# Turning tokens and attention by transfers inside SBUF and 32x32 transposes on VectorE, in the first phase of a decoder layer

## The reference

```python
q = elu(x @ Wq.T) + 1; k = elu(x @ Wk.T) + 1; v = x @ Wv.T        # 16 heads of 32
kv_state = einsum('bhnd,bhne->bhde', k, v)
attn_out = einsum('bhnd,bhde->bhne', q, kv_state) / max(q . k.sum(2), 1e-06)
local = xp[:, :-2] * conv_w[:, 0] + xp[:, 1:-1] * conv_w[:, 1] + xp[:, 2:] * conv_w[:, 2] + conv_b
out = (attn_out + local) @ Wp.T + bp
```

## Time and profile before

| | us |
|---|---|
| median of 3 runs (3150.09 to 3150.97) | 3150.3 |
| span of the profiled execution | 3149.0 |
| TensorE busy in it | 3109.7 |
| VectorE, ScalarE, GpSimd busy | 1781.6, 1298.2, 838.2 |
| one step of the first phase | 54.5 |

### The profile page before, as it was taken

The page is one execution under the profiler, slowest core; times in us unless marked ns, Lnnn a source line. Parts: engine busy times, 40 slices in busy tenths (PEclk is TensorE's granted clock), DMA queues, the critical chain, the costliest instruction groups (busy, mean ns, idle before and its releaser), DMA issues.

```text
span 3149.0 us, 41123 instructions
## 1 busy us (share of the span) xinstructions
PE 3109.7 (99%) x15828; PEld 2625.5 (83%) x15828; DVE 1781.6 (57%) x3901; ACT 1298.2 (41%) x2475; POOL 838.2 (27%) x699
## 2 busy tenths in 40 slices
PE   8999999999989999999999989999999999999999
PEld 7888888888878888888888878888888888888887
DVE  6666665766587877877787766232232232221355
ACT  4333333333456666766666653222222222221243
POOL 0101010110146666666666650000000000000144
PEclk9999999999999999999999999999999999999999
DMA  3121121212232112221221232000011000010386
GB/s 111 41 70 51 46 75 41 81 41 94 69 102 82 62 62 82 69 69 56 95 69 55 81 108 81 27 27 27 27 36 45 27 27 28 27 54 17 123 291 227
DMA packets 118802, 220.76 MB, mean 70 GB/s; under 512 B 7504, under 2 KB 13648, under 8 KB 118608
## 3 DMA queue, kind: packets, MB, share of 16 engines
q1 hardware_dynamic: 118608, 218.14, 20.4%
HBM read 152.06 MB, written 66.06 MB: 69 GB/s over the span
## 4 chain that ended last, share of the span: by engine, by line
PE 96%; DVE 2%; issue 1%; ACT 1%; DMA 0%; POOL 0%; SPq 0%; DVEq 0%; ACTq 0%
PE c_p L130 11%; PE c_p L132 11%; PE c_p L131 11%; PE a_p L130 6%; PE a_p L132 6%; PE a_p L131 5%; PE b_n L132 5%; PE b_n L130 5%; PE b_n L131 4%; PE b_t L1597 3%; PE d_p L132 2%; PE d_p L131 2%; PE d_p L130 2%; PE a_r L130 2%; PE a_r L132 2%; PE a_p L902 2%
## 5 line engine op out<-in xcount | busy, mean ns | idle before, releaser
L1217 POOL TENSOR_SCALAR b_soft<-b_soft,b_one_in_sum 128x512 f32<-128x512 f32 x256 | 401.4, 1569 | 299.6 <-DVE b_one_in_sum L1400 299.6
L1817 ACT ACTIVATE c_gate<-c_p,c_bias 128x512 f32<-128x512 f32 x180 | 124.2, 690 | 718.3 <-PE c_p L132 718.3
L1851 DVE TENSOR_TENSOR c_gate<-c_gate,c_gate 128x512 f32<-128x512 f32 x64 | 44.3, 692 | 524.0 <-ACT c_gate L1817 524.0
L1419 DVE TENSOR_TENSOR b_p_lo<-b_t,b_p_hi 128x512 fp32r<-128x512 f32 x256 | 175.2, 684 | 158.9 <-ACT b_p_hi L1274 156.3
L1265 ACT ACTIVATE b_soft<-b_soft,b_minus_top 128x512 f32<-128x512 f32 x256 | 185.2, 724 | 180.9 <-DVE b_minus_top L1411 176.3
L344 POOL TENSOR_TENSOR kept_scale<-c_ln_ve,minus_half 128x4 f32<-128x4 f32 x16 | 16.1, 1009 | 896.5 <-DVE c_ln_ve L336 896.5
L551 ACT ACTIVATE a_elu<-a_p 128x512 f32<-128x512 f32 x128 | 76.6, 599 | 353.1 <-PE a_p L132 353.1
L344 POOL TENSOR_TENSOR a_ln_sc<-a_ln_ve,minus_half 128x4 f32<-128x4 f32 x16 | 16.3, 1017 | 695.3 <-DVE a_ln_ve L336 695.3
L1274 ACT ACTIVATE b_p_hi<-b_t 128x512 fp32r<-128x512 f32 x256 | 151.9, 593 | 107.4 <-PE b_t L1597 107.4
L1411 DVE CUSTOM_DVE_ANT_0 b_soft<-b_l,b_mask_row 128x512 f32<-128x512 f32 x256 | 175.3, 685 | 0.0
L1597 PE MATMUL b_t<-ident,b_soft 128*128 128x128 f32 x1024 | 154.4, 273 | 12.4 <-DVE b_p_lo L1419 11.3
(11 more groups left out here) (286 smaller groups left out, 9622.8 us busy)
## 6 DMA issues: line engine op xcount, KB each, us to landing
a_res<-in_x SPq DMA_DIRECT2D x16, 1024.0 KB, 6.3
x<-a_res SPq DMA_DIRECT2D x16, 1024.0 KB, 5.3
b_mem<-in_ctx SPq DMA_DIRECT2D x16, 1024.0 KB, 5.4
b_x<-x SPq DMA_DIRECT2D x16, 1024.0 KB, 5.6
b_res<-x SPq DMA_DIRECT2D x16, 1024.0 KB, 5.6
x<-b_res SPq DMA_DIRECT2D x16, 1024.0 KB, 4.5
c_x<-x SPq DMA_DIRECT2D x16, 1024.0 KB, 5.9
d_x<-x SPq DMA_DIRECT2D x16, 1024.0 KB, 5.6
```

The costliest lines, as they stand in the source:

```text
L1217: pool.tensor_scalar(soft[:, at, :], soft[:, at, :], one_in_sum[:, at:at + 1], None, ALU.mult).then_inc(p_norm.sem, p_norm.unit)
L1419: dve.tensor_tensor(part.low, pT_bank[:, :].rearrange("p (i s) -> p i s", i=T), part.high_f32(), ALU.subtract).then_inc(p_lo.sem, p_lo.unit)
L1817: act.activation(gate[j % 2][i][:, :], gating.banks[(3 * j + i) % 6][:, :], ACT.Tanh if g == "c" else ACT.Sigmoid, bias=added[:, i, j:j + ...
```

## The change

Transposes on TensorE stay for the weights and the first item. The tokens of the later items and the attention of every item are turned in two moves. First sixteen transfers inside SBUF (`shuffle`), issued by SP, each of 32 partitions by 4 by 128 elements, exchange the 32-row blocks between the partition groups: the block of rows r and columns q goes to rows q. Then VectorE transposes squares of 32x32 inside each partition group (`turn_squares`), 128x512 in one instruction, four for an item. It reads every fourth element of a row, so the channels of a chunk are no longer neighbours: the channel of partition p and chunk c is 4p + c. So that weights and convolution parameters fit, TensorE reads the raw weights and the first item with the same stride (`interleaved`, `spread`). Transposed tokens lie in SBUF (`turned_f`) instead of in PSUM, from where ScalarE and VectorE read them. The transposed attention is written to `z_sum` and the local part added there in place. Both rotas lose the transposes' four places, and SP's stream gets the batches; in step 15 the loads of the second phase stand behind the attention's batch.

```diff
+def interleaved(row, c, chunks):
+
+    return row.rearrange("p (m c) -> p c m", c=chunks)[:, c]
+
...
         for o in range(self.C):
-            mm = pe.transpose(bank[:, o * P:(o + 1) * P], self.stages[i % len(self.stages)][:, o, c * P:(c + 1) * P], self.ident[:, :])
+            raw = self.stages[i % len(self.stages)]
+            part = interleaved(raw[:, o, :], c, self.C) if i in self.spread else raw[:, o, c * P:(c + 1) * P]
+            mm = pe.transpose(bank[:, o * P:(o + 1) * P], part, self.ident[:, :])
...
+    def shuffle(self, sp, to, src, event):
+
+        for q in range(4):
+            for r in range(4):
+                sp.dma_start(to[32 * q:32 * (q + 1), :, r * P:(r + 1) * P],
+                             src[32 * r:32 * (r + 1), :, q * P:(q + 1) * P]).then_inc(event.sem, event.unit)
+
+    def turn_squares(self, dve, to, src, c):
+
+        blocks = src[:, :, :].rearrange("p t (n c) -> p c (t n)", c=self.C)[:, c]
+        return dve.transpose(to[:, c, :], blocks)
...
-            att = sb("att", [P, BLOCKS, P])
+            att = sb("att", [P, T, D])
...
+            def shuffle(sp, b):
+                sp.wait_ge(N.normed.sem, N.normed.upto(b))
+                if b >= 2:
+                    sp.wait_ge(squared.sem, squared.upto(b - 2))
+                self.shuffle(sp, x_shuffled, x, shuffled)
...
-                         + [(kv_sb, g, 0) for g in range(2)] + [(tap2, c, -1) for c in range(C)], B)
+                         + [(kv_sb, g, 0) for g in range(2)], B)
...
-                          [(att_sb, g, 1) for g in range(GROUPS)] + [(z_f, c, 1) for c in range(C)] + [(x1_sb, t, 1) for t in range(T)], B)
+                          [(att_sb, g, 1) for g in range(GROUPS)] + [(x1_sb, t, 1) for t in range(T)], B)
...
-                    if new and new.b == B - 2:
+                    if old:
+                        sp.wait_ge(att_sb.sem, att_sb.upto(old.b))
+                        if old.b >= 1:
+                            sp.wait_ge(attT.sem, attT.upto(old.b - 1))
+                        self.shuffle(sp, att_shuffled, att, att_moved)
+                    if following(new, B):
+                        shuffle(sp, new.b + 1)
+                    if new and new.b == B - 1:
+                        sp.wait_ge(shuffled.sem, shuffled.upto(B - 2))
+                        self.b_load_mem(sp, 0)
+                        sp.wait_ge(tap2.sem, tap2.upto(B - 1))
+                        self.b_load_scale(sp)
+                        sp.wait_ge(squared.sem, squared.upto(B - 2))
                         self.b_load_output_weight(sp)
-                    if new and new.b == B - 1:
-                        sp.wait_ge(xT_ps.sem, xT_ps.upto(B - 1))
-                        self.b_load_mem(sp, 0)
-                        self.b_load_scale(sp)
...
                 def tokens_high(b, c):
-                    act.wait_ge(xT_ps.sem, xT_ps.upto(b, c))
+                    if b == 0:
+                        act.wait_ge(xT_ps.sem, xT_ps.upto(0, c))
+                    else:
+                        act.wait_ge(squared.sem, squared.upto(b - 1, c))
...
-                    act.activation(xT.high[:, c, :], first.bank(b - 1, TURN + c)[:, :], ACT.Copy).then_inc(xT_hi.sem, xT_hi.unit)
+                    act.activation(xT.high[:, c, :], turned(b, c), ACT.Copy).then_inc(xT_hi.sem, xT_hi.unit)
...
+                        dve.wait_ge(att_moved.sem, att_moved.upto(old.b))
                         for c in range(C):
-                            dve.wait_ge(attT_ps.sem, attT_ps.upto(old.b, c))
-                            dve.wait_ge(tap2.sem, tap2.upto(old.b, c))
                             if c >= 2 or old.b >= 1:
                                 dve.wait_ge(z_lo.sem, z_lo.upto(*divmod(old.b * C + c - 2, C)))
-                            dve.tensor_tensor(z_sum[c % 2][:, :], second.bank(s, TURNED + c)[:, :], local[old.par][:, c, :], ALU.add).then_inc(z_f.sem, z_f.unit)
+                            squares = att_shuffled[:, :, :].rearrange("p t (n c) -> p c (t n)", c=C)[:, c]
+                            dve.transpose(z_sum[c % 2][:, :], squares).then_inc(attT.sem, attT.unit)
+                            dve.wait_ge(attT.sem, attT.upto(old.b, c))
+                            dve.wait_ge(tap2.sem, tap2.upto(old.b, c))
+                            dve.tensor_tensor(z_sum[c % 2][:, :], z_sum[c % 2][:, :], local[old.par][:, c, :], ALU.add).then_inc(z_f.sem, z_f.unit)
                             if c >= 1:
                                 z_low(c - 1)
                         z_low(C - 1)
+                    if after:
+                        dve.wait_ge(shuffled.sem, shuffled.upto(after - 1))
+                        for c in range(C):
+                            self.turn_squares(dve, turned_f, x_shuffled, c).then_inc(squared.sem, squared.unit)
...
-                        if old:
-                            turn_att(c)
...
-                    if following(new, B):
-                        for c in range(C - 1 if old else C):
-                            turn_x(new.b + 1, c)
                     if new and old:
                         for t in range(T):
                             output(pe, old.b, t)
-                            if following(new, B) and t == 0:
-                                turn_x(new.b + 1, C - 1)
```

More of the change, by code:

```diff
@@ L357, in turn, with turn_interleaved @@
         return mm
+    def turn_interleaved(self, pe, bank, src, c):
+        for t in range(self.T):
+            mm = pe.transpose(bank[:, t * P:(t + 1) * P], interleaved(src[:, t, :], c, self.C), self.ident[:, :])
+        return mm
+    def shuffle(self, sp, to, src, event):
[6 more added lines that the diff above has]
+        return dve.transpose(to[:, c, :], blocks)
     def token_rows(self, dram, b):
@@ L410, in phase_a @@
             k = sb("k", [P, T, D])
+            self.place = Place(nc, self.base + 1024 * 166)
             kv_mask = sb("kv_mask", [P, 2, KVW])
@@ L959, in phase_b @@
             k_f = sb("k_f", [P, T, HD])
-            mask_u8 = [sb(f"mask_u8{i}", [P, S], U8) for i in range(2)]
+            mask_place = Place(nc, self.base + 1024 * 196)
+            mask_u8 = [mask_place.tile(f"b_mask_u8{i}", [P, S], U8) for i in range(2)]
             mask_row = [sb(f"mask_row{i}", [P, S]) for i in range(2)]
```

78 lines of the change are left out of this document (41 added, 37 removed).

## The result

The changed kernel took 3187.5 us (median of four runs, 3187.2 to 3189.7), the kernel before 3150.6 beside it. The ratio is 1.0117, with a 95% interval of 1.0103 to 1.0131: slower by 37 us, where I had forecast 46 us faster, 3105 us, and a range that ended at 3161. The profiled execution spans 3187.9 us, 38.9 more than before. Lines have moved: an attend is L896 now, a KV product L957, the second half of an elu L724, the z addition L794, its low part L785, the GpSimd additions L578, an issue of a 64 KB transfer L376.

A forecast was written before the change was run, and what follows sets the result against it. TensorE's instruction stream was taken to bound the steady steps. Terms: -53.6 us of transposes, +7.0 at the end, +1.0 at the start, so 3150.3 - 45.6 = 3104.7, rounded 3105 us; own range 3096 to 3113, 8-in-10 range 3096 to 3161.

The forecast's parts named there:

- What TensorE saves: Transposes leaving TensorE's stream save 3.58 us in each of steps 1 to 14, 53.6 us in all before the drain.
- The price of an issue: SP issues each 64 KB transfer in 0.47 us, so sixteen take 7.5 us and a batch 9.5 us with landing.
- The upper bound of 0.69: Slowest issue of a 64 KB transfer, if a 512-byte packet costs 87 ns: 3.8 us wait per step, 3161 us.
- The far case of 0.95: Transfers hardly overlap: 12.1 us wait per step, 3282 us; all of slower together has a chance of 0.22.
- The price of a transpose: A 32x32 transpose over 512 columns on VectorE takes 0.61 us, eight of them 4.9 us per step.
- the bound of 1.45: Upper bound in us for a VectorE transpose, what a normalisation takes while GpSimd runs.
- So I cost steps 1 to 15 at no new wait: The elu of Q ends at 36.1 us of the step, 2.0 us before the second KV group needs it.
- Rivals 1 and 2: First: steps wait for slow transfers, 3161 to 3282 us, chance 0.22. Second: slow transposes lose part of the gain, 3128, 0.16.
- The end: In the drain the attention batch and z chain have no products to hide under: costs 7.0 us.
- The start and step 15: Step 0 saves 1.64 us and strided reads cost 1 (0 to 5); step 15 saves 1.88 at no cost.
- the cover that I had taken as enough: Step 15: memory item lands near 27.5 us, ScalarE lets V copies through before Q units 2 and 3 need banks.
- At 0.67 the whole gain is gone: With 0.67 us per issue, the wait per step and the longer end use up the whole gain.

The follow-up runs named there:

- e12: e9 with one edit: GpSimd does its four residual additions behind the z chain instead of right behind its DMA issues; 3099.4 us, 0.9834.
- e3: The changed kernel with half the rows per transfer, 32 KB in 64 runs instead of 64 KB in 128; 3180.1 us, 1.0089.
- e10: The changed kernel with each 64 KB transfer over all 128 partitions, one run of 512 bytes on each; 3185.2 us, 1.0112.
- e4: The changed kernel with VectorE's transposes reading 512 neighbouring elements instead of every fourth of 2048; 3147.8 us, 0.9992.
- e2: The changed kernel with 24 identity transposes on TensorE behind the first KV group, to fill the wait; 3172.8 us, 1.0071.
- e11: The kernel before with only a stall added: VectorE does three idle transposes ahead of the elu steps of Q in steps 1 to 14; 3212.1 us, 1.0199.
- e8: The changed kernel with the elu steps of Q ahead of VectorE's token transposes and the last item's attention turned by TensorE; 3119.5 us, 0.9900.
- e5: The changed kernel with GpSimd issuing the last eight transfers of every batch, ahead of its norm power; 3163.7 us, 1.0038.
- e9: e8 with half of each batch issued by GpSimd, behind its norm power; 3143.9 us, 0.9979.

## Why the prediction was wrong, step by step

- **What TensorE saves.** Right. I took 3.58 us per step; e12 shows 54.50 - 50.79 = 3.71.
- **The price of an issue.** Wrong: 0.47 taken, 0.641 measured. It came from three loads that carry four times the data; e3 and e10 show that size and shape were not what to look at. The upper bound of 0.69, from the mean time of a packet, held it by luck: half the packets left the pitch as it was. The far case of 0.95 did not come; a transfer lands 2.1 us after its issue, so several are under way at once.
- **The price of a transpose.** Wrong: 0.61 taken, 1.01 to 1.12 measured, inside the bound of 1.45. The nearest row was a plain pass (an addition of a tile in PSUM and one in SBUF), but the operation reads with a stride, and e4 puts 0.38 us on that.
- **"So I cost steps 1 to 15 at no new wait".** This is the step that failed. Rivals 1 and 2 named the mechanism, the elu of Q queued behind the batch and the transposes. Each was priced with the other at its best value. With both prices as measured my own terms give an elu at 14.6 + 32 x 0.641 + 2.1 + 4.0 + 0.6 = 41.8, 3.7 us late; it was 3.1 us late in step 7, and 49.2 us in the 14 steps. I had it 2.0 us early.
- **The clock.** Not in the prediction at all. From the saved work and the measured waits, steps 1 to 14 should take 14 x (50.79 + 0.26) + 49.2 = 763.9 us, where 0.26 is the restart behind a wait (51.05 - 50.79). Step 1 takes 1.4 us more in either kernel. They take 790.7, so 25.4 us are the fallen clock. Without them the result would be 3162 us, past the end of my range and still slower than before: the waits alone turned the sign. e2 and e11 show that the wait causes the fall; why it follows some waits and not others is open.
- **The end.** 7.0 us taken, 12.4 measured to the mark. The batch takes 11.41 us to issue here, longer than in step 7, and is used 12.9 us after the attention is written instead of 9.5; the chain of z takes 9.8 us instead of 8.6. These 4.6 us are the whole difference up to the first transpose of b_x (31.1 against my 26.5). The last 0.8 fit the lower clock that TensorE has there, though no run separates it. e8, where the stretch is 43.9 us against 44.2 before, shows that nothing else is in it.
- **The start and step 15.** For the start I had 1.64 us saved and 1.0 spent, and the first attend is 0.64 us earlier: right in sum. The spent part is not all strided reads. From the first weight transposes, 0.36 us earlier than before, to the KV products, 0.33 later, they cost 0.7 us (a group of eight takes 1.12 instead of 1.03); the rest is a wait of 0.6 us for the masked KV state. Step 15 had 1.88 us saved and no cost, and lasts 52.82 us against 52.67. The memory item came 30.6 us into the step and not 27.5, ScalarE stood at its square, and TensorE waited 0.87 us for a V copy and 0.57 for an elu: the cover that I had taken as enough was not.
- **GpSimd's additions.** The 5.80 us normalisation stood in the rows as a price; I took it as given and did not ask what caused it, though it decided e5 and e9, beside the late norm power in e5.
- **The rivals' chances.** "At 0.67 the whole gain is gone" was worked out with a transpose of 0.61. Two unknown prices that add up in one wait need their joint case, and it lay beyond both.

## What to carry to other kernels

Small transfers are paid by the piece in the issuing queue: count issues, not bytes, and set the time of the whole batch against the first instruction that stands behind it in an engine's stream. If something has to wait for a batch, put what others need ahead of it; one such move was worth 57 us, and the second queue cost 24 us (e8 to e9) before GpSimd's additions had been moved from under the chain, and gained 20 after (e8 to e12). A wait on TensorE can cost more than its length, as the work behind it may run at half the clock; if it can't be avoided, filling it with matmuls that nobody needs gained 15 us here.

## What the runs showed of the hardware

- SP needs 0.64 us for each issue between SBUF tiles, for 32 KB or 64 KB, for 32 or 128 partitions (some batches 0.69 to 0.72, not explained). GpSimd needs 0.54; both at once work (SP then 0.72, e5).
- A 32x32 transpose on VectorE over 512 fp32 columns takes 0.71 us with neighbouring elements and 1.09 with a stride of 16 bytes. TensorE's own transposes read the same stride at 294 instead of 277 ns.
- TensorE's clock fell from 2.4 to 1.2 GHz behind a single wait of 3.0 us in otherwise full work, in 6 of 14 cases (e11), and not once when the wait was mostly filled with transposes that nobody needs (e2). It also fell behind 1.9 us (e4, two steps).
- One VectorE addition with both inputs in SBUF was held up 4.9 us by four GpSimd additions; elu steps with one input in PSUM were not held up at all (e12). Four normalisation steps over 512 columns take 5.80 us beside the same additions and 1.91 to 2.00 without them (e5, e9).
